# Attention with a feed-forward layer on one core: the causal mask of the diagonal blocks, applied to P by VectorE or added to the scores by TensorE

## The chip, the core and the metric

The kernel runs on one core of a Trainium2 chip. The metric is the device time of one execution in microseconds (us). TensorE is PE in the profile (its weight loads PEld), VectorE is DVE, ScalarE is ACT, GpSimd is POOL, and SyncE (SP) issues most transfers.

## What is computed

Inputs: x of 4 x 2048 x 512 in float32, four attention matrices and one chosen feed-forward matrix of 512 x 512, all with biases. The core of the reference:

```python
q = heads(x @ Wq + bq); k = heads(x @ Wk + bk); v = heads(x @ Wv + bv)   # 16 heads of 32
att = jnp.einsum('bhtd,bhsd->bhts', q, k) * (1.0 / math.sqrt(D))
att = jnp.where(mask[None, None, :, :] == 0, -jnp.inf, att)   # causal, and every 4th key left out
att = jax.nn.softmax(att, axis=-1)
y = jnp.einsum('bhts,bhsd->bhtd', att, v)
return y.transpose(0, 2, 1, 3).reshape(B, T, C) @ Wp + bp
...
x = x + _layernorm(_L0_attn_ref(_layernorm(x), ...))
x = x + _layernorm(_L0_ffn_ref(_layernorm(x), ...))   # x @ W[idx] + b[idx], idx from logits and u
```

## The kernel before

**Units, groups, blocks.** A unit u is 512 tokens of one batch; there are 16, and j = u % 4 is its place in the sequence. Of its 512 keys only 384 count, since every fourth key is masked out for all. A unit has 4 groups g of 4 heads a. The keys that a group sees are cut into blocks sb of 128 keys: 3j full blocks from earlier units, and 3 diagonal blocks, sb >= 3j. The diagonal ones start at column t0 = T0 = (0, 168, 336) of the unit's 512 tokens, so they are 512, 344 and 176 tokens wide, and only the first MW = 176 columns of each need a mask. Over all units there are 480 blocks for the groups, 192 of them diagonal.

**The steps of a group.** "peak" (L1160 on PE; L939, or L935 with the causal mask MASKM for the last chunk, on DVE) finds a row's greatest score, which "peaks" (L945 to L952) and "shift" (L1168, L823, a copy) put into two rows of QST, so that each score leaves PE with that maximum already subtracted. "score" (L1180) writes keys x tokens of one head into one of six PSUM banks of acc, and for a diagonal block a second matmul (L1184) adds a tile of the mask, MASKT, with the unit matrix IDB as weights. "exp" (L841, ACT) reads the bank and writes P, float32, in one of three buffers. "pv" (L1198) multiplies P with V for the four heads side by side into psO; "sum" (L1215) multiplies with ones into psU. For some of the full blocks POOL adds P into one buffer instead of a sum on PE (L717; L962 on DVE for the last groups). Then "out" (L849, ACT), "invert" (L969 to L973, DVE), "scale" and "olow" (L722, L726, POOL) and "ohigh" (L855, ACT) end the group. Projections (L1131 to L1136), layer norms (L907 to L918, L696) and the split into two float16 halves (L784, L703, L926, L708) of other units run between.

**What sets the order.** The class Order lists every step with its engine, a rank (a place in time), an estimated duration and what it needs, and plays a list schedule with them; from it come five fixed lists, one for each engine. Each engine runs its list in order and waits on semaphores. Banks (at most 4 for scores, 3 for peaks, 2 for projections, of 6 in all) are given in the same play. A change of one estimate or one need moves steps in all lists. P's buffers go round: a block's exp waits for pv and sum (or the addition) of the block that held its buffer, the next but one before it; a group's first block takes the third buffer, which then gathers the additions.

Of the kernel before, what the change touches and what calls it, by code (L numbers as in the profile page):

```python
# [51 lines left out]
class Order:  # L52
# [147 lines left out]
    def attend(self, u):  # L200
        add, j = self.add, u % self.NJ
        last = 3 * j + 2
        for g in range(4):
# [18 lines left out]
            for sb in range(last + 1):  # L222
# [3 lines left out]
                for a in range(4):  # L226
                    add("pe", at, w / 2.4 + (85 if sb >= 3 * j else 0), ("score", u, g, sb, a),
# [6 lines left out]
                    add("act", at, 0.98 * w + 70, ("exp", u, g, sb, a), [("pe", "score", u, g, sb, a)] + held)  # L234
                add("pe", at + 0.01, 1.75 * w + 60, ("pv", u, g, sb),
                    exps + ([("pe", "pv", u, g, sb - 1)] if sb else free) + [("act", "evac", ("v", u, a)) for a in range(3)])
            before = [("dve", "invert", *divmod(s - 1, 4))] if s else []
            for sb in sum_blocks(j):
                w = 512 if sb == "acc" else (512, 512, 344, 176)[max(sb - 3 * j + 1, 0)]
                done = ([(self.adder(u, g, a), "add", u, g, added(j)[-1], a) for a in range(4)] if sb == "acc" else  # L240
                        [("act", "exp", u, g, sb, a) for a in range(4)])
# [134 lines left out]
def sandwich_block(nc, x, Wq, bq, Wk, bk, Wv, bv, Wp, bp, Wf, bf, logits, uni, cf, cb, out):  # L376
# [21 lines left out]
    with ctx:  # L398
# [28 lines left out]
        CB = sb("CB", [128, 128 + 512 + 3 * MW], BF16)  # L427
# [24 lines left out]

        IDB = CB[:, 0:128]
        MASKM = CB[:, 128:640]
        MASKT = [CB[:, 640 + MW * i:640 + MW * (i + 1)] for i in range(3)]
# [10 lines left out]
        def sem(name):  # L466
# [5 lines left out]
        v_p, v_c, v_w, v_f, v_ln, v_n, v_q, v_m, v_s, v_o = (  # L472
            sem(n) for n in ("v_p", "v_c", "v_w", "v_f", "v_ln", "v_n", "v_q", "v_m", "v_s", "v_o"))
# [19 lines left out]
        def counted(steps, signals):  # L493
# [21 lines left out]
            "high": ("q", 1), "peak": ("m", 1), "peaks": ("m", 3), "add": ("s", 1), "invert": ("o", 3)}[s[0]])  # L515
# [43 lines left out]
        def resid_in(u, r):  # L559
            n = 4 * u + r  # L560
            return (d_r[n % 3], 16 * (n // 3 + 1)) if u < NU - 1 else (d_x[r], 16 * (len(PARTS[r]) * NU + 1))

# [295 lines left out]
        def _(e):  # L858
# [5 lines left out]
            for s in order.dve:  # L864
# [89 lines left out]
                elif kind == "add":  # L954
# [7 lines left out]
                    e.tensor_tensor(P[:, acc, a, :], P[:, acc, a, :], P[:, buf, a, :], ALU.add).then_inc(v_s, 1)  # L962
                elif kind == "invert":
# [132 lines left out]
        def _(e):  # L1096
            pe = Lean(e)
            for s in order.pe:
# [72 lines left out]
                elif kind == "score":  # L1171
# [5 lines left out]
                    if u:  # L1177
# [3 lines left out]
                                 start=True, stop=dg < 0)  # L1181
                    if dg >= 0:
                        pe.wait_ge(d_cb, 16)
                        i = e.matmul(bank(*s)[:, t0:t0 + MW], IDB, MASKT[dg], start=False, stop=True)  # L1184
                    i.then_inc(p_qk, 1)
                elif kind == "pv":
# [5 lines left out]
                    pe.wait_ge(a_e, exped(u, g, sb_))  # L1192
# [8 lines left out]
                elif kind == "sum":  # L1201
# [3 lines left out]
                    if sb_ == "acc":  # L1205
                        buf, t0 = p_acc[u, g], 0
                        for a in range(4):
                            pe.wait_ge(*summed(u, g, added(j)[-1], a))
                    else:
                        buf, t0 = p_buf[u, g, sb_], T0[sb_ - 3 * j] if sb_ >= 3 * j else 0  # L1210
                        pe.wait_ge(a_e, exped(u, g, sb_))
# [45 lines left out]
```

## Time and profile before

| | us |
|---|---|
| median of 3 runs | 2567.81 |
| lowest, highest | 2565.41, 2570.93 |
| the profiled execution | 2565.07 |
| its span, first to last instruction | 2563.3 |

The mean granted TensorE clock of the profiled execution is 0.986 of full speed. Busy times are unions of the durations of an engine's instructions; matmul durations are modelled and overlap, so PE's pace is read from the starts of its instructions. "Idle before" is the time in which an engine stood still just ahead of a group's instructions, with what released it. Durations of one group, when shapes are not kept apart, are means over all of them.

### The profile page before, as it was taken

The page shows a single profiled execution, that of the slowest core. Times are in us where ns is not written, and L with a number is a line of the kernel's source. Part 1 is how long each engine was busy: PE and PEld are TensorE (multiplying, and loading weights), DVE is VectorE, ACT ScalarE, POOL GpSimd, SP SyncE. Part 2 cuts the span into 40 slices and gives each one's busy share as a digit, 9 for nine tenths or more (in the row PEclk, how much of TensorE's full clock was granted, in tenths as well). Part 3 has the DMA queues.
Part 4 walks back from the last instruction along what each step waited for, and adds up shares of the span by engine and source line. Part 5 has one row for each costly group of instructions (what it writes and reads, how often), then busy time and mean ns, then how long its engine had stood idle before and what let it go on. Part 6 is the DMA issues. An engine that isn't in the chain of part 4 may idle for free.

```text
span 2563.3 us, 43166 instructions
## 1 busy us (share of the span) xinstructions
PE 2410.8 (94%) x15380; PEld 924.9 (36%) x15380; DVE 1804.7 (70%) x4820; ACT 1494.5 (58%) x2654; POOL 1427.6 (56%) x1318
## 2 busy tenths in 40 slices
PE   4899999998999999999999999999999999999986
PEld 2343333333343333333344343333234433333322
DVE  7767777777477777767567767767738766777764
ACT  5545566556655556557655565665665555565663
POOL 2235465665656365576754637557756454656623
PEclk9899999999999999999999999999999999999998
DMA  6223030111233231021122313002204131301001
GB/s 189 56 43 95 22 86 23 36 48 41 46 88 73 55 73 49 7 53 41 43 65 66 99 36 89 14 18 55 51 23 99 41 97 42 77 12 32 28 1 33
DMA packets 224352, 137.46 MB, mean 54 GB/s; under 512 B 146730, under 2 KB 196618, under 8 KB 224138
## 3 DMA queue, kind: packets, MB, share of 16 engines
q1 hardware_dynamic: 222310, 134.65, 20.8%
q8 instruction: 121, 1.98, 0.3%
q14 instruction: 93, 0.76, 0.1%
q10 hardware_dynamic: 1828, 0.07, 0.0%
HBM read 39.69 MB, written 16.78 MB: 22 GB/s over the span
## 4 chain that ended last, share of the span: by engine, by line
PE 59%; DVE 20%; POOL 7%; issue 6%; ACT 4%; DMA 2%; SPq 1%; ACTq 0%; POOLq 0%; DVEq 0%
PE psO L1198 12%; PE acc L1160 10%; PE acc L1180 9%; PE psU L1215 8%; PE acc L1131 6%; PE acc L1133 6%; PE acc L1132 6%; DVE MP L939 4%; POOL P L717 3%; ACT P L841 3%; DVE acc L935 3%; DVE STA L907 3%; DVE XR L918 2%; PE acc L1184 1%; DVE XB L918 1%
## 5 line engine op out<-in xcount | busy, mean ns | idle before, releaser
L841 ACT ACTIVATE P<-acc,EX 128x512 f32<-128x512 f32 (+2 forms) x1920 | 1076.6, 636 | 476.4 <-PE acc L1180 237.1
L939 DVE TENSOR_REDUCE MP<-acc 128x1 f32<-128x512 f32 (+1 forms) x1088 | 719.4, 679 | 220.3 <-PE acc L1160 217.1
L717 POOL TENSOR_TENSOR P<-P 128x512 f32<-128x512 f32 x546 | 683.7, 1281 | 151.0 <-ACT P L841 150.5
L1160 PE MATMUL acc<-KST,QST 96*128 96x512 f16 (+10 forms) x2112 | 584.0, 335 | 40.5 <-DVE MP L935 22.2
L935 DVE CUSTOM_DVE_ANT_0 acc<-acc,CB 128x96 f32<-128x96 f32 (+7 forms) x1024 | 450.3, 454 | 241.0 <-PE acc L1160 239.4
L1180 PE MATMUL acc<-QST,KST 98*128 98x512 f16 (+2 forms) x1920 | 571.7, 356 | 23.8 <-DVE MP L935 9.3
L1198 PE MATMUL psO<-P,V 128*32 128x512 f32 (+2 forms) x3840 | 464.8, 556 | 11.7 <-ACT P L841 9.3
L1160 PEld LDWEIGHTS acc<-KST,QST 96*128 96x128 f16 x2112 | 192.4, 97 | 393.1 <-issue 108.0
L722 POOL TENSOR_TENSOR SC<-SC 128x512 f32<-128x512 f32 x64 | 82.3, 1286 | 449.7 <-DVE SC L973 449.6
L1180 PEld LDWEIGHTS acc<-QST,KST 98*128 98x128 f16 x1920 | 179.3, 97 | 375.5 <-issue 154.5
L1215 PE MATMUL psU<-P,ONES 128*32 128x512 f32 (+2 forms) x2688 | 300.4, 519 | 0.0
L696 POOL TENSOR_TENSOR RR<-RR,NHALF 128x1 f32<-128x1 f32 x256 | 155.0, 607 | 224.8 <-DVE RR L911 224.0
L708 POOL TENSOR_TENSOR QKL<-SC,QKH 128x384 f16<-128x384 f32 (+1 forms) x128 | 133.7, 1044 | 158.1 <-DVE QKH L926 158.1
L1131 PE MATMUL acc<-XT,WH 128*128 128x384 f16 (+1 forms) x512 | 183.8, 359 | 15.1 <-DMA XT<-XF 6.1
L1133 PE MATMUL acc<-XT,WH 128*128 128x384 f16 (+1 forms) x512 | 182.2, 356 | 0.0
L1132 PE MATMUL acc<-XT,WL 128*128 128x384 f16 (+1 forms) x512 | 182.1, 356 | 0.0
L1184 PE MATMUL acc<-CB 128*128 128x176 bf16 x768 | 175.4, 241 | 0.0
L935 DVE DVE_READ_ACCUMULATOR2_ANT MP<- 128x1 f32 x1024 | 144.0, 141 | 0.0
L907 DVE BATCH_NORM_STATS2 STA<-YX 128x6 f32<-128x512 f32 x128 | 87.8, 686 | 76.3 <-ACT YX L813 59.5
L1198 PEld LDWEIGHTS psO<-P,V 128*32 128x32 f32 x3840 | 76.4, 108 | 169.7 <-ACT P L841 124.7
L1215 PEld LDWEIGHTS psU<-P,ONES 128*32 128x32 f32 x2688 | 83.3, 111 | 137.9 <-issue 135.3
L926 DVE CAST QKH<-SC 128x384 f16<-128x384 f32 (+1 forms) x128 | 63.9, 499 | 67.5 <-ACT SC L802 44.2
(140 smaller groups left out, 2832.7 us busy)
## 6 DMA issues: line engine op xcount, KB each, us to landing
QST<-QKH SPq DMA_DIRECT2D x128, 128.0 KB, 3.2
XR<-in_L_attn_x_dram SPq DMA_DIRECT2D x60, 256.0 KB, 3.0
out_dram<-XR SPq DMA_DIRECT2D x60, 256.0 KB, 2.1
KST<-QKH SPq DMA_DIRECT2D x128, 96.0 KB, 2.7
XB<-in_L_attn_x_dram SPq DMA_DIRECT2D x48, 252.0 KB
QST<-QKL SPq DMA_DIRECT2D x64, 128.0 KB, 3.3
KST<-QKL SPq DMA_DIRECT2D x64, 96.0 KB, 2.7
XB<-in_L_attn_x_dram SPq DMA_DIRECT2D x20, 256.0 KB, 3.5
```

Of the source, the lines that this page charges most:

```text
L717: e.tensor_tensor(P[:, acc, a, :], P[:, acc, a, :], P[:, buf, a, :], ALU.add).then_inc(g_s, 1)
L841: e.activation(P[:, p_buf[u, g, sb_], a, t0:512], bank(*step)[:, t0:512], ACT.Exp, scale=EX[:, 1:2]).then_inc(a_e, 1)
L935: e.tensor_tensor_reduce(out=ps, in0=ps, in1=MASKM[:, 512 - n:512], scale=1.0, scalar=-3.0e38, op0=ALU.add, op1=ALU.max, accum_out=maxima( ...
L939: e.tensor_reduce(maxima(u, g)[:, r, a, ci:ci + 1], bank(*s)[:, 0:n], AX.X, ALU.max).then_inc(v_m, 1)
L1131: e.matmul(o, lh, rh, start=kt == 0, stop=False)
L1132: e.matmul(o, ll, rh, start=False, stop=False)
L1133: i = e.matmul(o, lh, rl, start=False, stop=kt == 3 and bias is None)
L1160: i = e.matmul(bank(*s)[:, 0:n], QST[0:96, h, 128 * r:128 * r + 128], KST[0:96, h, c0:c0 + n], start=True, stop=True)
L1180: i = e.matmul(bank(*s)[:, t0:512], KST[0:98, h, 128 * sb_:128 * sb_ + 128], QST[0:98, h, t0:512], start=True, stop=dg < 0)
L1184: i = e.matmul(bank(*s)[:, t0:t0 + MW], IDB, MASKT[dg], start=False, stop=True)
L1198: i = e.matmul(psO[32 * a:32 * a + 32, t0:512], V[:, vb, 32 * h:32 * h + 32], P[:, p_buf[u, g, sb_], a, t0:512], start=first, stop=last)
L1215: i = e.matmul(psU[32 * a:32 * a + 32, t0:512], ONES[:, :], P[:, buf, a, t0:512], start=sb_ == blocks[0], stop=sb_ == blocks[-1])
```

## The change

The second matmul of a diagonal score is gone, and with it the unit matrix in CB. ACT takes the exponential of the unmasked scores. A new DVE step "mask" waits for the four exps of a diagonal block and then takes, in place, the minimum of P and the mask tile over the 176 columns of all four heads in one instruction (128 x 4 x 176); the mask tile now holds 0 where a key is in the future and 1.0e38 elsewhere, so that masked values become 0, even infinite ones. pv and sum of a diagonal block wait for this step. In the order, a diagonal score is 85 ns shorter and the mask is 800 ns long. The diff, without the names of the new semaphore v_k and its count:

```diff
@@ the order: attend @@
                 for a in range(4):
-                    add("pe", at, w / 2.4 + (85 if sb >= 3 * j else 0), ("score", u, g, sb, a),
+                    add("pe", at, w / 2.4, ("score", u, g, sb, a),
...
+                if sb >= 3 * j:
+                    add("dve", at, 800, ("mask", u, g, sb), exps)
+                    exps = [("dve", "mask", u, g, sb)]
                 add("pe", at + 0.01, 1.75 * w + 60, ("pv", u, g, sb),
                     exps + ([("pe", "pv", u, g, sb - 1)] if sb else free) + [("act", "evac", ("v", u, a)) for a in range(3)])
...
                 done = ([(self.adder(u, g, a), "add", u, g, added(j)[-1], a) for a in range(4)] if sb == "acc" else
-                        [("act", "exp", u, g, sb, a) for a in range(4)])
+                        [("dve", "mask", u, g, sb)] if sb >= 3 * j else [("act", "exp", u, g, sb, a) for a in range(4)])
@@ tiles @@
-        CB = sb("CB", [128, 128 + 512 + 3 * MW], BF16)
+        CB = sb("CB", [128, 512 + 3 * MW], BF16)
...
-        IDB = CB[:, 0:128]
-        MASKM = CB[:, 128:640]
-        MASKT = [CB[:, 640 + MW * i:640 + MW * (i + 1)] for i in range(3)]
+        MASKM = CB[:, 0:512]
+        MASKT = [CB[:, 512 + MW * i:512 + MW * (i + 1)] for i in range(3)]
@@ what pv and sum wait for @@
+        def weighed(u, g, sb_):
+
+            return (v_k, DV["mask", u, g, sb_]) if sb_ >= 3 * (u % NJ) else (a_e, exped(u, g, sb_))
@@ block.vector @@
+                elif kind == "mask":
+                    u, g, sb_ = s[1:]
+                    i = sb_ - 3 * (u % NJ)
+                    dv.wait_ge(a_e, exped(u, g, sb_))
+                    dv.wait_ge(d_cb, 16)
+                    o = P[:, p_buf[u, g, sb_], :, T0[i]:T0[i] + MW]
+                    e.tensor_tensor(o, o, MASKT[i].rearrange("p (a t) -> p a t", a=1).broadcast_to([128, 4, MW]), ALU.min
+                                    ).then_inc(v_k, 1)
@@ block.tensor, score @@
                     i = e.matmul(bank(*s)[:, t0:512], KST[0:98, h, 128 * sb_:128 * sb_ + 128], QST[0:98, h, t0:512],
-                                 start=True, stop=dg < 0)
-                    if dg >= 0:
-                        pe.wait_ge(d_cb, 16)
-                        i = e.matmul(bank(*s)[:, t0:t0 + MW], IDB, MASKT[dg], start=False, stop=True)
+                                 start=True, stop=True)
@@ block.tensor, pv and sum, both @@
-                    pe.wait_ge(a_e, exped(u, g, sb_))
+                    pe.wait_ge(*weighed(u, g, sb_))
@@ host constants @@
-    cb[:, 0:128] = _np.eye(128)
...
-        cb[:, 640 + 176 * i:640 + 176 * (i + 1)] = _np.where(
-            tok[128 * i:128 * i + 128, None] > t0 + _np.arange(176)[None, :], BIG, 0.0)
+        cb[:, 512 + 176 * i:512 + 176 * (i + 1)] = _np.where(
+            tok[128 * i:128 * i + 128, None] > t0 + _np.arange(176)[None, :], 0.0, -BIG)
```

## Rows read from the trace of the kernel before

In the views by window the columns are: stretch and its length in us, then for PE, PEld, DVE, ACT and POOL the busy us and the number of instructions, the granted share of TensorE's clock, the share of the DMA engines and their GB/s.

**Rows 1.** The page, part 1: busy us, share of the span, instructions.

```profile
PE 2410.8 (94%) x15380; PEld 924.9 (36%) x15380; DVE 1804.7 (70%) x4820; ACT 1494.5 (58%) x2654; POOL 1427.6 (56%) x1318
```

**Rows 2.** Busy time by engine in four units, j = 0, 1, 2, 3.

```profile
682.20:767.40 85.20, 81.91 (x574) 37.20 (x566) 64.10 (x205) 45.15 (x86) 45.37 (x46) 1.00 0.35 84
767.40:907.70 140.30, 137.04 (x903) 55.63 (x895) 100.83 (x288) 78.89 (x142) 66.86 (x65) 0.99 0.25 63
907.70:1083.30 175.60, 169.83 (x1085) 63.28 (x1081) 129.78 (x331) 105.48 (x187) 105.04 (x95) 1.00 0.18 45
1083.30:1299.60 216.30, 206.90 (x1302) 73.40 (x1298) 139.47 (x346) 136.84 (x239) 148.14 (x130) 0.99 0.16 41
```

**Rows 3.** Costliest groups by line: busy, mean ns | idle before, releasers.

```profile
L939 DVE TENSOR_REDUCE MP<-acc 128x1 f32<-128x512 f32 (+1 forms) x1088 | 719.4, 679 | 220.3 <-PE acc L1160 217.1
L935 DVE CUSTOM_DVE_ANT_0 acc<-acc,CB 128x96 f32<-128x96 f32 (+7 forms) x1024 | 450.3, 454 | 241.0 <-PE acc L1160 239.4
...
L1160 PE MATMUL acc<-KST,QST 96*128 96x512 f16 (+10 forms) x2112 | 584.0, 335 | 40.5 <-DVE MP L935 22.2 <-DVE MP L939 8.4 <-ACT SC L802 1.8
...
L1198 PE MATMUL psO<-P,V 128*32 128x512 f32 (+2 forms) x3840 | 464.8, 556 | 11.7 <-ACT P L841 9.3
```

**Rows 4.** The same with shapes kept apart, PE.

```profile
L1184 PE MATMUL acc<-CB 128*128 128x176 bf16 x768 | 175.4, 241 | 0.0
...
L1180 PE MATMUL acc<-QST,KST 98*128 98x344 f16 x256 | 73.3, 314 | 4.5 <-DVE MP L935 2.2 <-ACT P L841 1.9
...
L1180 PE MATMUL acc<-QST,KST 98*128 98x176 f16 x256 | 54.7, 242 | 1.1
...
L1168 PE MATMUL acc<-IDH,MHL 128*8 128x128 f16 x256 | 24.9, 220 | 7.4 <-DVE MHL L952 7.4
```

**Rows 5.** Instructions in order of time, PE: start us, us, then as above.

```profile
1294.86 0.24 PE L1184 MATMUL acc<-CB 128*128 128x176 bf16 x1
1294.94 0.31 PE L1180 MATMUL acc<-QST,KST 98*128 98x344 f16 x1
```

**Rows 6.** Single lines: duration ns min/median/max of their instructions.

```profile
L962 DVE TENSOR_TENSOR P<-P x30: 681/686/1172, 2445.3 to 2507.8; 128x512 f32<-128x512 f32 x30
...
L717 POOL TENSOR_TENSOR P<-P x546: 1252/1270/1750, 167.4 to 2465.1; 128x512 f32<-128x512 f32 x182
```

**Rows 7.** Groups with shapes kept apart, DVE, two widths of L935.

```profile
L935 DVE CUSTOM_DVE_ANT_0 acc<-acc,CB 128x512 f32<-128x512 f32 x64 | 44.3, 693 | 40.5 <-PE acc L1160 40.5
...
L935 DVE CUSTOM_DVE_ANT_0 acc<-acc,CB 128x352 f32<-128x352 f32 x64 | 33.5, 523 | 3.5 <-PE acc L1160 3.5
```

**Rows 8.** In order of time, DVE and POOL, late in the last unit.

```profile
2448.09 2.97 POOL L717 TENSOR_TENSOR P<-P 128x512 f32<-128x512 f32 x2 [0.92 <-ACT P L841]
...
2449.20 0.71 DVE L962 TENSOR_TENSOR P<-P 128x512 f32<-128x512 f32 x1 [0.44 <-ACT P L841]
...
2450.44 1.17 DVE L962 TENSOR_TENSOR P<-P 128x512 f32<-128x512 f32 x1
```

**Rows 9.** L918: min/median/max of one form, and two forms' means.

```profile
L918 DVE TENSOR_SCALAR XB<-XB,MV,RR x68: 529/547/5960, 11.0 to 2558.7; 128x512 f32<-128x512 f32 x68
...
L918 DVE TENSOR_SCALAR XB<-XB,MV,RR 128x512 f32<-128x512 f32 x68 | 66.9, 985 | 16.8 <-POOL RR L696 16.8
...
L918 DVE TENSOR_SCALAR XR<-XR,MV,RR 128x512 f32<-128x512 f32 x60 | 44.1, 735 | 2.4 <-POOL RR L696 2.3
```

**Rows 10.** Busy time in a diagonal stretch, j = 3, and behind it.

```profile
1239.30:1250.60 11.30, 11.09 (x92) 4.41 (x91) 7.88 (x26) 5.70 (x13) 2.20 (x3) 1.00 0.00 0
1250.60:1285.30 34.70, 34.28 (x216) 12.05 (x216) 9.96 (x37) 26.82 (x45) 27.29 (x23) 1.00 0.15 41
```

**Rows 11.** In order of time, the last group's last block.

```profile
2514.87 1.30 ACT L841 ACTIVATE P<-acc,EX 128x176 f32<-128x176 f32 x4 [1.87 <-PE acc L1184]
...
2516.23 0.51 PE L1198 MATMUL psO<-P,V 128*32 128x176 f32 x8 [0.92 <-ACT P L841]
```

**Rows 12.** Busy time in a stretch of the first unit.

```profile
72.00:90.00 18.00, 13.76 (x95) 5.30 (x94) 17.18 (x50) 8.88 (x15) 0.55 (x1) 0.83 0.00 1
```

More of the change, by code:

```diff
@@ L471, in sandwich_block @@
             sem(n) for n in ("a_p", "a_k", "a_w", "a_c", "a_e", "a_o", "a_m", "a_q", "a_v", "a_y"))
-        v_p, v_c, v_w, v_f, v_ln, v_n, v_q, v_m, v_s, v_o = (
-            sem(n) for n in ("v_p", "v_c", "v_w", "v_f", "v_ln", "v_n", "v_q", "v_m", "v_s", "v_o"))
+        v_p, v_c, v_w, v_f, v_ln, v_n, v_q, v_m, v_s, v_k, v_o = (
+            sem(n) for n in ("v_p", "v_c", "v_w", "v_f", "v_ln", "v_n", "v_q", "v_m", "v_s", "v_k", "v_o"))
         g_ln, g_p, g_q, g_s, g_o, g_r = (sem(n) for n in ("g_ln", "g_p", "g_q", "g_s", "g_o", "g_r"))
@@ L514, in sandwich_block @@
             "fold": ("f", 17 if s[-1] == 2 else 1), "stats": ("ln", 3), "norm": ("n", 1),
-            "high": ("q", 1), "peak": ("m", 1), "peaks": ("m", 3), "add": ("s", 1), "invert": ("o", 3)}[s[0]])
+            "high": ("q", 1), "peak": ("m", 1), "peaks": ("m", 3), "add": ("s", 1), "mask": ("k", 1), "invert": ("o", 3)}[s[0]])
         GP = counted(order.gp, lambda s: {
@@ L1210, in _ @@
                         buf, t0 = p_buf[u, g, sb_], T0[sb_ - 3 * j] if sb_ >= 3 * j else 0
-                        pe.wait_ge(a_e, exped(u, g, sb_))
+                        pe.wait_ge(*weighed(u, g, sb_))
                     if n:
@@ L1241 @@
     BIG = -1.0e38
-    cb = _np.zeros((128, 128 + 512 + 3 * 176), _np.float32)
-    cb[:, 0:128] = _np.eye(128)
+    cb = _np.zeros((128, 512 + 3 * 176), _np.float32)
     key = _np.arange(384)
     tok = 4 * (key // 3) + key % 3
-    cb[:, 544:640] = _np.where(tok[None, 0:96] > _np.arange(128)[:, None], BIG, 0.0)
+    cb[:, 416:512] = _np.where(tok[None, 0:96] > _np.arange(128)[:, None], BIG, 0.0)
     for i, t0 in enumerate((0, 168, 336)):
-        cb[:, 640 + 176 * i:640 + 176 * (i + 1)] = _np.where(
-            tok[128 * i:128 * i + 128, None] > t0 + _np.arange(176)[None, :], BIG, 0.0)
+        cb[:, 512 + 176 * i:512 + 176 * (i + 1)] = _np.where(
+            tok[128 * i:128 * i + 128, None] > t0 + _np.arange(176)[None, :], 0.0, -BIG)
     give("cf", _np.eye(128, dtype=_np.float32))
```

## The prediction, made before the changed kernel was run

> **What bounds the kernel now.** I read the page's busy shares first, then the busy time of each engine in single units, then PE's own stretch in order of time. PE is busy for 2410.8 us of 2563.3, DVE for 1804.7, ACT for 1494.5, POOL for 1427.6 [rows 1]. Single units say the same with less averaging: in one with j = 0 PE is busy for 81.9 of 85.2 us and DVE for 64.1, in one with j = 3 PE for 206.9 of 216.3 and DVE for 139.5; those with j = 1 and 2 are alike, with PE at 137.0 of 140.3 and 169.8 of 175.6 [rows 2]. So PE sets the pace and DVE is second, nearest to it in the units with j = 0 (75% of the time, from 64.1 / 85.2). When DVE stands idle it is mostly for PE: 239.4 us before L935 and 217.1 us before L939, both released by L1160 [rows 3]. The reader should see in this that time taken off PE has a chance to be time off the kernel, and that work put on DVE fits into gaps, if its place in time does not hold PE up.
>
> **What is removed.** 768 matmuls of 176 columns with their weight loads (L1184), four for each of 192 diagonal blocks [rows 4]. Their duration of 241 ns is not their price: matmuls overlap. In order of time a mask matmul starts at 1294.86 and the next instruction at 1294.94, 0.08 us later [rows 5]. A second way gives the same: a score of 344 columns takes 314 ns and one of 176 takes 242, thus 0.43 ns a column and 75 ns for 176 [rows 4]. I take 0.078 us. 768 x 0.078 = 60 us of PE's stream, 3.7 us in each of the 16 units, 0.94 us in each of the 64 groups. The shortening of CB and the smaller load of the constants (one transfer at the start) cost and give nothing that I can see: that transfer is one of those at the start, and the rest of the sum does not hang on it.
>
> **What is added.** 192 tensor_tensor with a minimum on DVE, 128 x 704 elements, both inputs in SBUF. The nearest row is L962, the same kind with 512 elements: 686 ns median, 681 the least [rows 6]. The slope per element comes from L935, 693 ns for 512 and 523 for 352: 1.06 ns [rows 7]. 686 + 192 x 1.06 = 890 ns undisturbed. That the second operand is repeated over the four heads has no row of its own; L935 reads the same bf16 tile at this rate, so I put nothing on it. With the least duration of L962 it is 0.88 us, the low bound; a gain below that is excluded, since no row of DVE with two streams takes less than 1.06 ns an element.
>
> The disturbed price is higher. One L962 took 1.17 us where the one before it took 0.71 and the median is 0.69, while POOL was in its additions, and two of POOL's additions took 2.97 us together, against 2.54 at their median of 1.27 each [rows 6, 8]. So a DVE instruction with two SBUF operands and a POOL one hold each other up. The high bound is a mask that waits out a whole addition of POOL, 0.89 + 1.27 = 2.2 us. The Trainium skill, SBUF — State Buffer, section "Who interferes with whom", says that a DVE instruction with two SBUF inputs and a GpSimd instruction that reads SBUF block each other, the later one until the earlier one has ended. By that rule, the trace agrees (1.17 us in place of 0.69), and it speaks against the change: it would put a mask that meets POOL anywhere up to the high bound. How often it happens is to be read from L918, the DVE group whose durations are spread most: median 547 ns, with means from 985 down to 735 ns over its four large forms, so 0.2 to 0.4 us of waiting on average [rows 9]. I take 0.3, so 1.2 us for a mask, with bounds 0.88 and 2.2. DVE gets 192 x 1.2 = 230 us more: 2035 us, 80% of the new time. POOL gets at most the same 0.9 us for each mask that it meets; in a diagonal stretch of a unit with j = 3 it is busy for only 2.2 of 11.3 us, against 27.3 of 34.7 in the stretch behind it [rows 10]. POOL's cost I take as nothing there; where the cover is gone it is in the high end.
>
> **What is moved: the wait.** pv and sum of a diagonal block now wait for the mask instead of for the four exps, so each is released later by a handoff and 0.9 to 1.2 us plus whatever stands ahead of the mask on DVE. Behind the mask on DVE queue the peaks L939 and L935, which empty the three banks that PE's L1160 needs, and "high", which POOL's "rest" and the copies of q and k need. Behind pv on PE queues everything that the order has put there. Who waits for pv in turn: the exps of the next block but one, by the ring of P buffers, and "out". The planned order places pv after the mask's estimated end (800 ns and 220 of lag), so the wait costs only what the plan misjudges or cannot fill.
>
> What a planned handoff costs PE is bounded by rows. The low one: PE stood idle for 11.7 us before 480 pv blocks, of which 9.3 us for exps, 0.02 us a block [rows 3]. The next: before L1168, where PE waits for a short serial DVE result, 7.4 us in 64 places, 0.12 us each [rows 4]. The high one: nothing fills the wait and PE loses all of it, as at the end of the last group, where the exps that start at 2514.87 take 1.30 us and pv starts at 2516.23, when they have ended [rows 11]; there it is the mask's full 0.9 us and a handoff. I take 0.12, since this too is a wait for DVE in a queue with peaks: 192 x 0.12 = 23 us. The high bound for all, 192 x 0.9 = 173 us, would need PE to have no other work in any diagonal stretch. Against it stands the stretch at 1239.3, where PE is busy for 11.1 of 11.3 us while ACT has 5.7 and DVE 7.9: it holds much more than the diagonal block's own work [rows 10].
>
> **Where the gain does not count.** Unit 0: between 72 and 90 us DVE is busy for 17.2 of 18 us [rows 12], so there masks cost DVE's time at once, and PE's 3.7 us give nothing. I put 4 us of loss for some three masks that fall into it. Units 4, 8, 12 (j = 0): DVE gets 64.1 + 12 x 1.2 = 78.5 us for a length that would be 81.5 without the mask matmuls; an in-order engine at 96% can't follow, so I count no gain: 3 x 3.7 = 11 us lost from it. The end: 1 us for the last mask.
>
> **The sum.** -60 + 4 (unit 0's matmuls) + 11 (j = 0) = -45 in the other 12 units; their 144 masks at 0.12 us give +17; start and end +5. -23 us. Against the profiled execution's own 2565.07 us (span 2563.3) that is 2542; against the median of 2567.8 it is 2545. I forecast 2545.
>
> **The rivals.** (a) *Forecast*, 2545, own range 2530 to 2558; chance 0.40. (b) *The mask hides fully*, handoffs at 0.02 us: -60 + 4 + 5 + 4 with the units j = 0 gaining too, -47 to -55, about 2517. For it: pv's present waits are nearly all filled, and the diagonal stretch leaves DVE 3.4 of 11.3 us free. Against it: DVE in j = 0. Chance 0.20. (c) *Slower: the masks hold up the peaks.* The mechanism is in the diagonal stretches: a mask of 1.2 us, or one that waits for late exps, keeps the three peak banks full, L1160 and the scores behind it stall, and pv comes late as well. It decides from 60 / 192 = 0.31 us of PE idle for each mask; at 0.5 us the sum is 96 - 60 = +36, 2604. Its strongest form is a mask that always waits out an addition of POOL: at 2.2 us a mask, a unit with j = 0 has 64.1 + 26.4 = 90.5 us of DVE, over its 85.2 by 5.3 us, thus +21 us in four units, and one with j = 1 has 100.8 + 26.4 = 127.2 us in a length of 136.6, 93%. Against it: mean waits at L918 are 0.2 to 0.4 us, not 1.3. Chance 0.26. (d) *No change*, 2563 to 2573: as (c), at just about 0.31 us a mask, or the planned order, which is made anew with other costs for a score and a mask, packs the other work worse by as much. Chance 0.14. That the change doesn't do what it says I can nearly exclude: the matmuls and their waits are gone from the code; the one part left is that the order moves elsewhere, which lies in (d).
>
> The range: 2510 (just beyond b) to 2592 (two thirds of c). It leaves out the far ends of (b) and of (c), some 0.2 together. 0.2% of this time, 5 us, is about what a measurement can tell from no change. Faster by more: 0.40 + 0.20 = 0.60; within it 0.14; slower 0.26.
>
> **What would show each step.** L1184 gone, and no form with 176 bf16 columns on PE; PE's busy time down by some 60 us, not by the 175 us that the group's durations add up to. A DVE group of 192 tensor_tensor with a median of 0.89 and a mean near 1.2 us; DVE's share near 80%. "Waits" with PE before L1198 for the mask: 3 to 25 us in total if (a) or (b), over 60 if (c). PE idle before L1160 for L935 and L939, 30.6 us now [rows 3], stays below 50 in (a) and doubles in (c). The units with j = 0 at 85 us or so, those with j = 1 to 3 shorter by 2 us each. POOL's additions at a mean near 1.29. I am wrong if the mask takes over 1.5 us on average, if j = 0 units grow by over 3 us, or if the other units don't shrink.

## The result and the profile after

The changed kernel takes 2580.93 us (median of 6 runs, 2575.67 to 2583.06), the kernel before 2567.78 in the same runs: ratio 1.005, 95% interval 1.0035 to 1.0065. It is 13 us slower. The forecast was 2545, with 2510 to 2592 as the range and 0.26 for slower.

The profiled execution of the changed kernel has a span of 2573.2 us, against 2563.3. Line numbers are those of the changed kernel: peaks are L1174 on PE and L945 and L941 on DVE, scores L1194, exp L847, pv L1209, the shift L1182, the mask L975, POOL's additions L723. Part 1 of its page, to be held against [rows 1]:

```profile
PE 2375.8 (92%) x14612; PEld 873.8 (34%) x14612; DVE 1984.1 (77%) x5012; ACT 1488.0 (58%) x2654; POOL 1455.7 (57%) x1318
```

PE lost 768 instructions but only 35 us of busy time where 60 were expected, and its idle time rose from 152.5 to 197.4 us (span less busy time). DVE gained 179 us. The same by units, j = 0 to 3, the answer to [rows 2] (same columns):

```profile
682.10:770.10 88.00, 81.63 (x533) 34.67 (x529) 77.76 (x227) 46.07 (x88) 48.33 (x46) 0.98 0.34 84
770.10:908.60 138.50, 131.25 (x839) 50.78 (x835) 112.72 (x300) 76.88 (x140) 67.37 (x64) 1.00 0.23 59
908.60:1085.70 177.10, 169.68 (x1053) 61.35 (x1046) 143.39 (x345) 105.96 (x187) 108.77 (x96) 0.99 0.18 46
1085.70:1301.80 216.10, 205.35 (x1247) 70.39 (x1238) 150.06 (x348) 136.22 (x239) 148.89 (x130) 0.98 0.16 41
```

The unit with j = 0 is 2.8 us longer, the one with j = 2 is 1.5 longer, those with j = 1 and 3 are 1.8 and 0.2 shorter. These are single units, and where one is cut from the next matters as much as these differences: cut at each unit's first pv and summed over the four units of a kind, the change is +0.8, -1.9, +4.7 and +6.3 us for j = 0 to 3. PE is no longer busy nearly throughout: 131.3 of 138.5 us with j = 1, where it had 137.0 of 140.3. Who waits shows in the groups by line, the answer to [rows 3]:

```profile
L945 DVE TENSOR_REDUCE MP<-acc 128x1 f32<-128x512 f32 (+1 forms) x1088 | 718.3, 678 | 153.5 <-PE acc L1174 150.8
L941 DVE CUSTOM_DVE_ANT_0 acc<-acc,CB 128x96 f32<-128x96 f32 (+7 forms) x1024 | 449.9, 453 | 187.2 <-PE acc L1174 185.0
...
L1174 PE MATMUL acc<-KST,QST 96*128 96x512 f16 (+10 forms) x2112 | 597.2, 336 | 35.8 <-DVE MP L941 15.0 <-DVE MP L945 11.0 <-ACT YX L819 1.3
L1209 PE MATMUL psO<-P,V 128*32 128x512 f32 (+2 forms) x3840 | 468.2, 559 | 49.9 <-DVE P L975 43.3 <-ACT P L847 4.2 <-ACT SC L855 0.4
```

PE's idle time before pv went from 11.7 to 49.9 us, and 43.3 of it is for the mask. DVE's own waits for peaks shrank from 457 us [rows 3] to 336: its idle time was used, but as the runs below show, at a price. The mask itself, from the view of its line (duration ns min/median/max, then who waited for it, us in total and times):

```profile
L975 DVE TENSOR_TENSOR P<-P,CB x192: 873/885/2011, 76.7 to 2526.4; 128x704 f32<-128x704 f32 x192
...
  PE psO L1209: 43.3, 53
```

One mask in order of time, in the unit behind the last of those above (start us, us, engine, line):

```profile
1304.80 1.26 ACT L847 ACTIVATE P<-acc,EX 128x512 f32<-128x512 f32 x2
...
1306.11 0.40 DVE L941 CUSTOM_DVE_ANT_0 acc<-acc,CB 128x192 f32<-128x192 f32 x1
...
1306.42 0.89 DVE L975 TENSOR_TENSOR P<-P,CB 128x704 f32<-128x704 f32 x1
...
1306.65 1.68 POOL L732 TENSOR_TENSOR OTL<-SC,OTH 128x512 f16<-128x512 f32 x1 [0.27 <-ACT OTH L861]
...
1307.63 1.07 PE L1209 MATMUL psO<-P,V 128*32 128x512 f32 x8
```

The exps end at 1306.06, the mask begins behind a peak at 1306.42 and ends at 1307.31, pv begins at 1307.63. From the last exp to pv it takes 1.6 us. POOL's "olow", which starts under the mask, takes 1.68 us; the median of the 64 is 1.16. Over all 192 masks, worked out from the trace and the order, a mask begins 0.94 us after its last exp, lasts 1.03 us, and pv follows 0.38 us later: 2.35 us on average.

### The profile page after: what moved, and what is told of

Its sections match the earlier page's. It is cut to its first block, busy times and chain, and to the rows that moved or that the text cites. A ratio compares the mean times of both kernels' runs of the same rounds, so it can differ in the third digit from the quotient of the medians.

```text
span 2573.2 us, 41838 instructions
## 1 busy us (share of the span) xinstructions
PE 2375.8 (92%) x14612; PEld 873.8 (34%) x14612; DVE 1984.1 (77%) x5012; ACT 1488.0 (58%) x2654; POOL 1455.7 (57%) x1318
## 4 chain that ended last, share of the span: by engine, by line
PE 54%; DVE 28%; POOL 7%; ACT 5%; issue 4%; DMA 1%; SPq 1%; ACTq 0%; POOLq 0%; DVEq 0%
PE psO L1209 12%; PE acc L1174 9%; PE acc L1194 8%; PE psU L1226 7%; PE acc L1145 6%; DVE MP L945 5%; PE acc L1146 5%; PE acc L1147 5%; DVE acc L941 5%; ACT P L847 4%; DVE P L975 3%; DVE STA L913 3%; POOL P L723 3%; DVE XR L924 3%; DVE XB L924 1%
## 5 line engine op out<-in xcount | busy, mean ns | idle before, releaser
L847 ACT ACTIVATE P<-acc,EX 128x512 f32<-128x512 f32 (+2 forms) x1920 | 1071.7, 639 | 420.0 <-PE acc L1194 343.1
L945 DVE TENSOR_REDUCE MP<-acc 128x1 f32<-128x512 f32 (+1 forms) x1088 | 718.3, 678 | 153.5 <-PE acc L1174 150.8
L723 POOL TENSOR_TENSOR P<-P 128x512 f32<-128x512 f32 x546 | 684.0, 1281 | 104.7 <-ACT P L847 104.5
L1174 PE MATMUL acc<-KST,QST 96*128 96x512 f16 (+10 forms) x2112 | 597.2, 336 | 35.8 <-DVE MP L941 15.0
L1194 PE MATMUL acc<-QST,KST 98*128 98x512 f16 (+2 forms) x1920 | 566.2, 358 | 34.5 <-ACT P L847 12.0
L941 DVE CUSTOM_DVE_ANT_0 acc<-acc,CB 128x96 f32<-128x96 f32 (+7 forms) x1024 | 449.9, 453 | 187.2 <-PE acc L1174 185.0
L1209 PE MATMUL psO<-P,V 128*32 128x512 f32 (+2 forms) x3840 | 468.2, 559 | 49.9 <-DVE P L975 43.3
L1174 PEld LDWEIGHTS acc<-KST,QST 96*128 96x128 f16 x2112 | 195.5, 97 | 420.3 <-issue 116.1
L1194 PEld LDWEIGHTS acc<-QST,KST 98*128 98x128 f16 x1920 | 178.4, 98 | 384.9 <-issue 137.4
L1226 PE MATMUL psU<-P,ONES 128*32 128x512 f32 (+2 forms) x2688 | 306.2, 527 | 0.0
L702 POOL TENSOR_TENSOR RR<-RR,NHALF 128x1 f32<-128x1 f32 x256 | 169.8, 665 | 200.5 <-DVE RR L917 199.7
L975 DVE TENSOR_TENSOR P<-P,CB 128x704 f32<-128x704 f32 x192 | 197.5, 1029 | 29.5 <-ACT P L847 29.1
L1209 PEld LDWEIGHTS psO<-P,V 128*32 128x32 f32 x3840 | 80.0, 109 | 224.2 <-DVE P L975 93.7
L941 DVE DVE_READ_ACCUMULATOR2_ANT MP<- 128x1 f32 x1024 | 143.0, 140 | 0.0
L932 DVE CAST QKH<-SC 128x384 f16<-128x384 f32 (+1 forms) x128 | 69.1, 540 | 67.6 <-ACT SC L802 46.7
```

Source lines behind the costliest of these rows:

```text
L847: e.activation(P[:, p_buf[u, g, sb_], a, t0:512], bank(*step)[:, t0:512], ACT.Exp, scale=EX[:, 1:2]).then_inc(a_e, 1)
L941: e.tensor_tensor_reduce(out=ps, in0=ps, in1=MASKM[:, 512 - n:512], scale=1.0, scalar=-3.0e38, op0=ALU.add, op1=ALU.max, accum_out=maxima( ...
L945: e.tensor_reduce(maxima(u, g)[:, r, a, ci:ci + 1], bank(*s)[:, 0:n], AX.X, ALU.max).then_inc(v_m, 1)
L975: e.tensor_tensor(o, o, MASKT[i].rearrange("p (a t) -> p a t", a=1).broadcast_to([128, 4, MW]), ALU.min).then_inc(v_k, 1)
L1174: i = e.matmul(bank(*s)[:, 0:n], QST[0:96, h, 128 * r:128 * r + 128], KST[0:96, h, c0:c0 + n], start=True, stop=True)
L1194: i = e.matmul(bank(*s)[:, t0:512], KST[0:98, h, 128 * sb_:128 * sb_ + 128], QST[0:98, h, t0:512], start=True, stop=True)
```

## The experiments

All ratios are to the kernel before, run beside on the same chip; one hundredth is 25.7 us. Differences between two ratios carry 0.002 to 0.003 either way, 5 to 8 us. Eight kernels (e10, e17, e5, e2, e1, e14, e13, e15) keep the changed kernel's five lists exactly and alter only what is issued or waited for, so that they can be compared step by step. In all others the lists are the old ones or are made anew.

**e10, the changed kernel's lists without masks.** The step "mask" stays in the order and issues nothing; pv and sum wait for the exps. It leaves the causal mask of the diagonal blocks out.

```diff
                 elif kind == "mask":
-                    ...
-                    e.tensor_tensor(o, o, MASKT[i]..., ALU.min).then_inc(v_k, 1)
+                    continue
```

> The changed kernel's lists without any mask instruction and with pv and sum waiting for the exps; the causal mask of the diagonal blocks is left out. Between this and the kernel without masks in lists of its own (0.985 of before) lies what it costs to have planned for masks. The kernel with narrow masks stood at 0.989, so it should lie at 0.985 to 0.988, 2522 to 2532. If it is at 0.993 or above, the lists and not DVE's work cost the better part, and the sum I make of e1, e5 and e2 falls.

Measured: 2510.46 us, ratio 0.9787 (0.977 to 0.9803). That is 55 us below the kernel before. Expected was 0.985 to 0.988: a miss on the good side, since I had taken these lists to be worse than lists made for a kernel without masks. They are better. This run is the floor from which the next ones are counted.

**e17, the same lists with TensorE's mask matmuls.** The kernel before, planned as the changed one; DVE issues no mask, and all of the masking is done as before.

```diff
-                    add("pe", at, w / 2.4 + (85 if sb >= 3 * j else 0), ("score", u, g, sb, a),
+                    add("pe", at, w / 2.4, ("score", u, g, sb, a),
...
+                if sb >= 3 * j:
+                    add("dve", at, 800, ("mask", u, g, sb), exps)
+                    exps = [("dve", "mask", u, g, sb)]
```

> The lists of the changed kernel, with TensorE's mask matmuls in place of the DVE masks (the mask step stands in the order only, and issues nothing); all of the mask is applied. If the 60 us of PE stream count in full in these lists: 0.9787 + 0.0234 = 1.002 of the kernel before. If part of 0.9787 is that these lists are better packed, and matmuls are worth 30 us as between e4 and e12: 0.990, and then this kernel beats the one before and the changed one. The price of the removed matmuls in the changed kernel is the difference to e10_lists_alone either way.

Measured: 2547.31 us, ratio 0.9922 (0.9909 to 0.9936). So the new lists alone make the kernel before 20 us faster, and 768 mask matmuls cost (0.9922 - 0.9787) x 2567.8 = 35 us, not 60. It is near the second of the two cases expected, 0.990. Part 1 of e17's page:

```profile
PE 2402.6 (94%) x15380; PEld 931.4 (37%) x15380; DVE 1814.0 (71%) x4820; ACT 1489.1 (59%) x2654; POOL 1434.5 (56%) x1318
```

The same part for e10:

```profile
PE 2357.2 (94%) x14612; PEld 872.7 (35%) x14612; DVE 1804.6 (72%) x4820; ACT 1486.5 (59%) x2654; POOL 1433.6 (57%) x1318
```

The order is the same instruction for instruction, yet 35 us came off the span (2545.5 to 2510.3) for 45 us of PE's busy time: PE's idle time rises by 10 us, from 142.9 to 153.1. Why the busy time fell by 45 and not by the 60 of the stream is not shown; matmul ends are modelled.

**e5, DVE work for which nobody waits, with one SBUF input.** The lists again; in the mask's place DVE takes a maximum over the same 128 x 704 of P. The exps that reuse the buffer wait for it, pv and sum don't. Each of these DVE instructions also waits for the one before it, here and in e2, e13 and e14. Nothing is masked.

```diff
-                    e.tensor_tensor(o, o, MASKT[i]..., ALU.min).then_inc(v_k, 1)
+                    e.tensor_reduce(SCR[:, :], o, AX.X, ALU.max).then_inc(v_k, 1)
```

> As e2_mask_unwaited (2560 us, 36 us above the kernel without masks in the new order, 2524), same lists, same places, but the 192 DVE instructions read the same 128 x 704 of P with one input in SBUF (a maximum over it, written to four numbers of which nobody takes note), so nothing is masked. It should take the same 0.88 us, but without a second SBUF operand. If POOL and DVE holding each other up is what makes the DVE load dear, the mean falls to 0.89 from 0.98 and the time to 2530 to 2545. If it is DVE's queue (peaks that wait behind masks), the time stays within 8 us of 2560.

Measured: 2544.77 us, ratio 0.9935 (0.9913 to 0.9956), 38 us above e10. That is the edge of what the first theory expected, and 15 us below the second. Where PE waits shows in its peaks and scores. In e10:

```profile
L1190 PE MATMUL acc<-QST,KST 98*128 98x512 f16 (+2 forms) x1920 | 564.1, 357 | 34.9 <-ACT P L847 12.3 <-DVE MP L941 6.9 <-DMA QST<-MROW 3.7
```

And in e5:

```profile
L1178 PE MATMUL acc<-KST,QST 96*128 96x512 f16 (+10 forms) x2112 | 600.2, 336 | 39.9 <-DVE MP L944 16.7 <-DVE MP L948 13.0 <-ACT YX L820 1.3
L1198 PE MATMUL acc<-QST,KST 98*128 98x512 f16 (+2 forms) x1920 | 566.9, 357 | 41.0 <-DVE MP L944 12.5 <-ACT P L850 11.8 <-DVE MP L948 4.3
```

PE's idle for DVE's peaks, ahead of its own peaks, goes from 18.7 (the line of e10 is under e15) to 29.7 us, and ahead of scores from between 6.9 and 10.6 (the list names three causes) to 16.8, while nothing waits for the added instructions but exps. In all, PE's idle time rises by 18 us and its busy time by 13; the last section has the clock's part in this. The kernel e5 is to be compared with is e2, which follows.

**e2, the same with two SBUF inputs.** The real minimum over P and a mask tile, written to a tile of bfloat16 that nobody reads; otherwise as e5.

```diff
-            return (v_k, DV["mask", u, g, sb_]) if sb_ >= 3 * (u % NJ) else (a_e, exped(u, g, sb_))
+            return a_e, exped(u, g, sb_)
...
-                    e.tensor_tensor(o, o, MASKT[i]..., ALU.min).then_inc(v_k, 1)
+                    e.tensor_tensor(SCR, o, MASKM[:, 0:MW]..., ALU.min).then_inc(v_k, 1)
```

> The changed kernel with every list and place kept and all of DVE's mask work, but pv and sum wait for the exps alone: the mask reads P and writes to a tile that nobody reads, so the causal mask of the diagonal blocks is left out; only the exp that reuses the buffer waits for the mask. If the wait costs, PE's idle time before pv falls from 49.9 us to about 12 and the time to 2515 to 2535. If DVE's load costs, it stays at 2560 to 2580, with PE idle before the peaks and scores as in the changed kernel.

Measured: 2560.28 us, ratio 0.9989 (0.9976 to 1.0002), 52 us above e10. PE's idle before pv is down to 7.4 us, as it would be if the wait had been the cost, but the time is where the load was to put it. The DVE group of e5 (ns min/median/max):

```profile
L980 DVE TENSOR_REDUCE SCR<-P x192: 869/879/887, 77.5 to 2495.5; 128x4 f32<-128x704 f32 x192
```

And that of e2:

```profile
L980 DVE TENSOR_TENSOR CB<-P,CB x192: 876/887/2005, 76.7 to 2513.2; 128x704 bf16<-128x704 f32 x192
```

The medians are 8 ns apart, but with one input no instruction takes over 887 ns, and with two some take up to 2005. The means are 879 and 1034 ns: 0.155 us of waiting in each, and POOL's busy time rises from 1432.8 to 1456.2 us. Both are the cost of two engines holding each other up.

**e1, short masks with the full wait.** The mask takes 4 columns of each head; place and waits as in the changed kernel. Most of the masking is left out.

```diff
-                    o = P[:, p_buf[u, g, sb_], :, T0[i]:T0[i] + MW]
+                    o = P[:, p_buf[u, g, sb_], :, T0[i]:T0[i] + 4]
```

> The changed kernel with every list, wait and place of the order kept; the mask takes 4 columns of each head in place of 176, so that most of the causal mask is left out. A mask should take about 0.2 us in place of 1.03, DVE some 160 us less. The changed kernel is at 2581 us, the kernel before at 2568, and 60 us of PE stream are saved. If DVE's load is what costs (peaks and everything else behind the masks), the time falls to about 2515 to 2525. If the mere handoff over DVE's queue costs (the mask starts 0.94 us after the last exp on average, whatever it takes itself), it falls by less than half of the 73 us: 2545 to 2570, and PE's idle time before pv stays above 25 us (49.9 in the changed kernel, 11.7 before).

Measured: 2534.49 us, ratio 0.9886 (0.9858 to 0.9915), 25 us above e10. The short mask takes 315 ns on average, and PE's idle before pv is 20.2 us. That is neither the 25 or more of the handoff theory nor the 2515 to 2525 us of the load theory. Both parts are there.

**e14 and e13, half and double the load.** As e5, over 80 columns of each head (0.48 us), and with each instruction issued twice (1.76 us).

```diff
-                    o = P[:, p_buf[u, g, sb_], :, T0[i]:T0[i] + MW]
+                    o = P[:, p_buf[u, g, sb_], :, T0[i]:T0[i] + 80]
```

```diff
+                    e.tensor_reduce(SC2[:, :], o, AX.X, ALU.max)
                     e.tensor_reduce(SCR[:, :], o, AX.X, ALU.max).then_inc(v_k, 1)
```

> As e5_one_input, over 80 columns of each head in place of 176: about 0.48 us each in place of 0.88, 92 us of DVE in all. In proportion: 21 us above 0.9787, so 0.987. If DVE's spare time takes in a small load for nothing and only the rest costs: 0.979 to 0.983. If the place costs and not the length: 0.991 or more.

> As e5_one_input (0.9935 of the kernel before, 38 us above the same lists without masks at 0.9787), with each of the 192 DVE instructions issued twice, so some 340 us of DVE in place of 169. In proportion: another 38 us, 1.008. If DVE's spare time is what is used up, the second half costs much more than the first: 1.015 to 1.04. If the cost were a fixed one for each place, 0.994 to 0.998.

Measured: 2528.08 us, 0.9871 (0.985 to 0.9892), in proportion as expected, and 2613.53 us, 1.0203 (1.0186 to 1.022), within the case where the second half costs more. With e10 and e5 that is a curve, DVE us added against time added: 92 gives 22, 169 gives 38, 337 gives 107. Up to 169 us DVE work costs 0.23 of its length, and beyond it 0.41. The line through the first two points meets no load at 2 us, which is within the noise: neither a free portion nor a fixed price is seen, although DVE stands idle for over a quarter of the time in e10. Less than 92 us of such work was not measured.

**e15, the same work at one other set of places.** As e10, but three reductions of 0.88 us for each group stand ahead of peaks, over a constant tile. In the order there is no step for them there.

```diff
                 elif kind == "peak":
+                    if a == 1 and ci == 0 and r < 3:
+                        e.tensor_reduce(SCR[:, r, :], ONES[:, :]...broadcast_to([128, 22, 32]), AX.X, ALU.max
+                                        ).then_inc(v_k, 1)
```

> The same lists without masks; three DVE reductions over 704 elements in each group (the same 0.88 us, 192 in all) stand in front of a peak of another group, spread over the group's time, and not behind the exps of the diagonal blocks. They read a constant tile, and nothing waits for them. If the load costs wherever it stands: 0.990 to 0.997, as e5_one_input. If the place behind the exps (the wait for the exp, with the peaks behind it held) is what costs: 0.980 to 0.986. DVE waits of its own for the exps were 30 us in e5_one_input.

Measured: 2592.69 us, ratio 1.0132 (1.0111 to 1.0153), 89 us above e10, for the same 169 us of DVE. Both cases expected were lower, at most 0.997. So the place behind the exps is not what costs; at these places the work costs over twice as much. PE's peaks in e10, by line:

```profile
L1170 PE MATMUL acc<-KST,QST 96*128 96x512 f16 (+10 forms) x2112 | 593.9, 335 | 29.1 <-DVE MP L945 10.6 <-DVE MP L941 8.1 <-ACT YX L819 1.3
```

And in e15:

```profile
L1178 PE MATMUL acc<-KST,QST 96*128 96x512 f16 (+10 forms) x2112 | 600.1, 336 | 63.9 <-DVE MP L953 30.4 <-DVE MP L949 23.9 <-ACT YX L820 1.3
```

PE's idle for DVE's peaks trebles, from 18.7 to 54.3 us. One difference between e5 and e15 is the place, the other that the order had a step of 800 ns at the first and none at the second. A third is that DVE stood idle for exps before some of e5's, 30 us in all, and before none of e15's. I did not run them apart, so that the planned room is what makes the one cheaper is only argued.

**e16, a fourth bank for the peaks.** `"psM": 3` becomes `"psM": 4` in the changed kernel's limits, which makes all lists anew.

> The changed kernel with one limit of the order changed: peaks may hold 4 of the 6 PSUM banks in place of 3, so PE may run one peak further ahead of DVE. If the three banks are what lets DVE's masks hold up PE, the PE idle before peaks and scores falls and the time is 10 to 25 us below the changed kernel, 0.995 to 1.001. If scores then lack banks, it is level or slower: 1.003 to 1.012.

Measured: 2578.12 us, ratio 1.0071 (1.0054 to 1.0088). No gain; this is the second case expected. PE's idle before pv falls to 36.2 us, the idle before the peaks rises to 40.4. That three banks are the bound is not borne out, but since all lists are made anew, this one run can't exclude that a fourth bank helps and worse lists hide it.

**e3, e4 and e12, lists around the matmuls.** e3 is the kernel before without L1184; e4 is e3 planned without the 85 ns; e12 is the kernel before, with its matmuls, in e4's lists. e3 and e4 leave the mask of the diagonal blocks out. The diff is e4's; e3 has its second part alone, e12 its first.

```diff
-                    add("pe", at, w / 2.4 + (85 if sb >= 3 * j else 0), ("score", u, g, sb, a),
+                    add("pe", at, w / 2.4, ("score", u, g, sb, a),
...
-                                 start=True, stop=dg < 0)
-                    if dg >= 0:
-                        pe.wait_ge(d_cb, 16)
-                        i = e.matmul(bank(*s)[:, t0:t0 + MW], IDB, MASKT[dg], start=False, stop=True)
+                                 start=True, stop=True)
```

> The kernel before without its 768 mask matmuls, nothing in their place, and the lists as they were; the causal mask of the diagonal blocks is left out. It measures the term of 60 us. If all of PE's stream counts: 2508. If the 40 us of unit 0 and of the units with j = 0 are bound otherwise, as the forecast had it: 2520 to 2525. If PE's saved time is mostly lost to waits for DVE's peaks: above 2540.

> As the run before it, but the order is planned with the 85 ns for the mask matmul taken out, so all lists are made anew. If a new plan is worth nothing by itself it is within 5 us of the run with the old order. If the old plan with its wrong times packs worse, it is 5 to 20 us faster; if the plan packs worse by chance, slower by as much. The difference is a measure of how much of a few tens of us can come from the lists alone.

> The kernel before with all its mask matmuls, but planned as if they cost nothing, so with the lists of e4_no_mask_new_order. Without the matmuls these lists were 15 us faster than the old ones. If they are better as such, this kernel is 10 to 15 us faster than the one before, about 0.995. If they were only better because they fit a kernel without the matmuls, it is level or slower: 1.000 to 1.006.

Measured: e3 0.9909 (0.9882 to 0.9935), e4 0.9849 (0.982 to 0.9878), e12 0.9957 (0.994 to 0.9973). Without its matmuls the kernel gains 23 us in the old lists; in e4's they are worth 28 us. e3, 2539.48 us, missed the 2520 to 2525 of the forecast's own reasoning by 15 us, and lies at the edge of the third case, where most of PE's saved time goes into waits for peaks; its idle before them is 50.0 us against 40.5. e4 and e12 came out as the second and the first of their cases. e12 is 11 us faster than the kernel before, with the same instructions: an estimate that was true by the trace (85 ns planned, 78 measured) gave worse lists than one of zero.

**e6, e9 and e11, the mask's estimate and rank.** In the changed kernel, e6 plans the mask at 1300 ns, e9 gives it a rank lower by 5 so that it goes ahead of peaks, e11 does this with 1050 ns.

```diff
-                    add("dve", at, 800, ("mask", u, g, sb), exps)
+                    add("dve", at - 5, 1050, ("mask", u, g, sb), exps)
```

> The changed kernel with one number of the order changed: the mask is planned at 1300 ns in place of 800, where it measured 1029 and started 0.94 us after the last exp. If pv's 50 us of idle come from a plan that is too hopeful, PE's idle before pv falls to 20 to 30 us and the time by 10 to 25 us, to 2550 to 2565. If DVE's load decides, PE's idle only moves to the peaks and scores and the time stays within 8 us of 2575.

> The changed kernel, where the mask's rank is lowered by 5, so that the order puts each mask on DVE as soon as its four exps have been planned to end, ahead of peaks that are ready too. In the changed kernel the mask started 0.94 us after the last exp. If the place in DVE's queue is what makes the masks dear, that wait falls to about 0.6 us, PE's idle before pv from 50 to 30 us and the time by 10 to 20 us. If it is DVE's load, peaks only wait in the mask's place and the time stays within 8 us of the changed kernel's 1.005 of before.

> As e9_mask_first, with the mask planned at 1050 ns, near the 1029 measured. If rank and a true estimate work together, PE's idle before pv is at 15 to 25 us and the time at 1.000 of the kernel before or below. With DVE's load deciding: 1.002 to 1.008.

Measured: e6 1.0062 (1.0045 to 1.0079), e9 1.0061 (1.0045 to 1.0078), e11 1.0011 (1.0001 to 1.002). In e6 PE's idle before pv falls to 15.6 us and the one before the peaks rises to 64.8:

```profile
L1174 PE MATMUL acc<-KST,QST 96*128 96x512 f16 (+10 forms) x2112 | 599.6, 337 | 64.8 <-DVE MP L945 31.7 <-DVE MP L941 17.1 <-ACT YX L819 3.8
```

PE's wait moved from pv to the peaks, and the time stayed. e9 agrees, with the place: the mask starts 0.52 us after the last exp in place of 0.94, and nothing is won. Both came out as the load theory had them. Both together take 10 us off, to the level of the kernel before and not below, between the two cases expected. As each of these kernels has lists of its own, and lists alone move the time by up to 20 us, they support the reading and do not prove it.

**e7, masks on DVE for j = 1 and 3 alone.** The other units keep the matmuls. To use TensorE's tile the mask is a scalar_tensor_tensor here, (tile >= -1) times P; 96 of them, 981 ns each on average.

```diff
+DVE_MASKS = (1, 3)
...
-                if sb >= 3 * j:
+                if sb >= 3 * j and j in DVE_MASKS:
```

> The DVE mask in the units with j = 1 and 3 only, TensorE's mask matmuls in those with j = 0 and 2. In the changed kernel the units with j = 1 and 3 were 4 and 9 us shorter in all than before, those with j = 0 and 2 were 9 and 10 us longer. If what a mask costs is set by how full DVE is in its unit, this one takes the shorter of each: 10 to 18 us below the kernel before, about 2548 where that has 2562. If the plan's luck decides and not the unit, it is within 5 us of the kernel before. The mask is written as another DVE instruction here (tile >= -1, times P), to use TensorE's mask tile; I expect the same duration.

Measured: 2569.3 us, ratio 1.0021 (1.0011 to 1.0032). The 10 to 18 us expected below the kernel before did not come: it is not the shorter of each, and that DVE's share in a unit decides on its own is not borne out. The units' differences on which that was built depend on where units are cut, the lists changed in all units, and this one run can't tell how much of the time is theirs.

**e8, masks on POOL.** As a multiplication with 0 or 1, planned at 1760 ns.

```diff
-                    add("dve", at, 800, ("mask", u, g, sb), exps)
+                    add("gp", at, 1760, ("mask", u, g, sb), exps)
```

> The changed kernel with the mask as a multiplication with 0 or 1 on POOL instead of the minimum on DVE, planned at 1760 ns (704 elements at the pace of its additions, 1.27 us for 512). DVE has its load of before, POOL gets some 336 us more, 70% in place of 56%. If DVE's load is what cost, the PE idle before the peaks and scores returns to that of the kernel without masks and what is left is the longer wait of pv: 2530 to 2560. If the latency between exp and pv decides, 1.75 us in place of 1.03 makes it slower than the changed kernel: 2580 to 2610.

Measured: 2583.71 us, ratio 1.0069 (1.005 to 1.0088). A mask takes 1.53 us on average. Part 1 of its page:

```profile
PE 2403.4 (93%) x14612; PEld 880.5 (34%) x14612; DVE 1851.3 (72%) x4820; ACT 1487.6 (58%) x2654; POOL 1717.7 (66%) x1510
```

The time is in the range of the latency case, yet PE's idle before pv is only 13.7 us, so the latency is not what it shows. DVE's busy time rises by 47 us over e10 though it has no mask. That POOL holds it up is the likely reason and not shown, and the lists are others. It is as slow as with masks on DVE.

## Why the prediction was wrong

The change falls into terms that add up, each the difference of two runs; all but the first are within one set of lists:

| step | runs | ratio | us |
|---|---|---|---|
| the lists made anew | before to e17 | 1 to 0.9922 | -20 |
| mask matmuls away | e17 to e10 | 0.9922 to 0.9787 | -35 |
| 0.88 us of DVE for each block, one SBUF input | e10 to e5 | 0.9787 to 0.9935 | +38 |
| the second SBUF input | e5 to e2 | 0.9935 to 0.9989 | +14 |
| pv and sum wait for it | e2 to changed | 0.9989 to 1.005 | +16 |
| sum | | | +13 |

**What bounds the kernel.** PE was read rightly as the pace, but "work put on DVE fits into gaps" is the sentence that failed. DVE's gaps were read as spare time, since they end on PE's peaks [rows 3]. They are one half of taking turns: PE fills a bank, DVE empties it, and a DVE that comes 0.9 us late makes PE late, at peaks and then at scores. e14, e5 and e13 show the cost, 0.23 us and more for each us of DVE, and the rows of e10, e5 and e15 show where PE waits.

**What is removed.** Columns and pace were right: 0.078 us for each, 60 us of stream. The step from stream to time was not. I took off 15 us for unit 0 and the units with j = 0 and counted the other 45 in full; measured were 35 in the changed kernel's lists, 28 in e4's and 23 in the old ones.

**What is added.** The undisturbed mask was right, 890 ns against 885 (and 879 for one input); the least was 873, just under the low bound of 0.88 us. The disturbed one was too dear, 1.2 us against 1.03; 40 of the 192 took over 1 us, the longest 2.01, within my high bound of 2.2. The 0.3 us of waiting came from L918, whose first mean includes one instruction of 5.96 us, and no run ties its waits to POOL; the mask's own were 0.14. The Trainium skill, SBUF — State Buffer, section "Who interferes with whom", has a DVE instruction with two SBUF inputs contend with GpSimd's reads, and one with at most one such input not, some faster modes aside. The trace agrees: in the same place a mean of 1034 ns and a longest of 2005 with two, 879 and 887 with one. POOL's additions kept their mean of 1281 ns, and what it lost fell on others of its instructions. The sum had nothing for the second input, which is 14 us.

The step that failed most is the next one: DVE's 230 us were costed at nothing outside unit 0 and the units with j = 0. The time for DVE's work is 38 us, and 52 with the second input. The sum had 5 us for it at the start and the end, beside the 15 us of gain that it withheld and that are counted above. So the miss of 36 us, from -23 to +13, is +47 here, +10 in what is removed, -1 in the wait and -20 in the lists. That the units with j = 1 to 3 would be 2 us shorter each was wrong too: in the single units shown they were 1.8 us shorter, 1.5 longer and 0.2 shorter, with DVE busy for 81%, 81% and 69% of them, and by the other cut none of these kinds is shorter by more than 0.5 us a unit. "The other units don't shrink" was a mark of being wrong, and it came.

**The wait.** 0.12 us a mask, 23 us in the whole and 17 in the sum, against 0.08 us and 16 between e2 and the changed kernel, give or take 5. The nearest row was a good guide, though the two kernels also differ in where the minimum is written. Seen in PE's idle time before pv, which grew by 38 us, the wait looks dearer; but part of that idle only stands in place of other idle, which e6 shows.

**The lists.** I named "the planned order, which is made anew" in rival (d) as a loss only. It was a gain of 20 us, which hid more than half of the loss: within these lists the same substitution costs 33 us (e17 to the changed kernel). What it costs within the lists of before was not run. That 2581 us still lies inside the range of 2510 to 2592 is luck: without the 20 us it would be 2601.

**The rivals.** (c) is nearest in mechanism: masks keep DVE from the peaks. Its price was put at 0.31 us a mask to be level; with 60 us of gain that was the right form, and with the 35 us measured the balance lies at 0.18. The masks cost 68 us, 0.35 each. What (c) named as its place, full banks, was not borne out: a fourth bank gave nothing (e16, in lists of its own). The marks I set did not tell the rivals apart: PE's wait before pv for the mask is 43.3 us, between the 25 of (a) and (b) and the 60 of (c), and idle before the peaks for DVE went down from 30.6 to 26.0, as in (a), while the time went as in (c).

## What to carry to other kernels

An engine that is idle for a quarter of the time, waiting for the engine that sets the pace, may have no spare time if the two take turns over a few buffers, as here: measure what a dummy instruction of the right length costs there, before moving work. Where an order is planned by a list schedule, hold the lists fixed and change one thing at a time; here a change of lists alone moved the same kernel by 20 us, more than the whole result. The fastest kernel of this study that does all of the work is e17, 0.9922 (0.9909 to 0.9936): TensorE's masks in lists planned for something else; e12 with 0.9957 is second.

## What was not expected

The granted TensorE clock is lower in the kernels that put this work on DVE or POOL, and this may be part of the price. The view of the cores for the changed kernel:

```profile
core 0: 2573.2 us, clock 0.982
```

The same for e10:

```profile
core 0: 2510.3 us, clock 0.986
```

And for e2:

```profile
core 0: 2559.5 us, clock 0.978
```

The kernel before had 0.986 as well, e17 0.986, e5 0.983, and e8 had 0.970. PE's idle time alone does not set it: e7 has 0.976 with 167.3 us of idle, e16 0.985 with 189.6. With two levels, 1.2 and 2.4 GHz, a mean of 0.986 is 2 x 0.014 x 2563.3 = 72 us at the lower one, and 0.978 is 2 x 0.022 x 2559.5 = 113 us. At most half of the 41 us between them could be lost on PE.

The medians over all runs are 0.9865 for e10, 0.9825 for e5, 0.978 for e2 and 0.979 for the changed kernel. By the same working the clock's part, an estimate, is at most 10 of the 38 us between e10 and e5, at most 12 of the 14 between e5 and e2, and nothing of the 16 behind it. For e13, with 0.9755, it is at most 18 of the 69 us over e5, so its steeper price is not the clock's alone. The ten runs of e2 go from 2563.0 us at 0.976 to 2554.3 at 0.982, 1.5 us for each 0.001; at that rate the parts would be 6 and 7 us. So most of what DVE's work costs is not the clock's, but about half of what the second SBUF input costs may be, and the runs do not tell these apart.

Open is how far each list is good or bad by chance. Planning 85, 0 or 0 and 800 ns for steps that exist or not gave 1, 0.9957 and 0.9922 for one and the same work, and no row of a trace explains the ranking.
